# Linear attention with a gated feed-forward: queries over the whole array, and a first chunk with its own order of work

## The chip, the cores and the metric

The kernel runs on one core of one Trainium2 chip. The metric is the device time of the whole kernel in microseconds; lower is better. A core has TensorE (matrix products and transposes), VectorE, ScalarE, GpSimd and SyncE, each with its own instruction stream; in the profile they are PE, DVE, ACT, POOL and SP, and PEld is TensorE's weight load. They meet at semaphores only.

## The reference

x has shape (8, 1024, 256) in fp32. One layer is computed:

```python
xn = layernorm(x)                                    # over the 256 channels
q, k, v = (split_heads(xn @ W.T) for W in (Wq, Wk, Wv))   # 16 heads of 16
q, k = elu(q) + 1, elu(k) + 1
kv_state = einsum('bhnd,bhne->bhde', k, v)
k_state = k.sum(axis=2)
attn = einsum('bhnd,bhde->bhne', q, kv_state) / maximum(einsum('bhnd,bhd->bhn', q, k_state), 1e-6)
local = xp[:, :-2] * conv_w[:, 0] + xp[:, 1:-1] * conv_w[:, 1] + xp[:, 2:] * conv_w[:, 2] + conv_b
y = (attn + local) @ Wp.T + bp
h = silu(xn @ wg.T) * (xn @ wu.T)                    # 768 wide, integer weights times 1/127
out = x + y + h @ wd.T
```

## The kernel before

The 8 x 1024 tokens are worked off in 16 chunks of 512 tokens (4 tiles of 128), two chunks (c = 0, 1) to a batch b. The instruction stream of every engine is written out by hand as one `step(b, c, attend, ahead)` per chunk; b = 2 to 6 are a loop. `past` is false in the very first step only, `attend` is true from batch 1 on, `ahead` in all steps but the last.

For the precise products each fp32 operand is split into a high and a low fp16 half, and three products are summed (high x high, low x high, high x low). The weights are first scaled by powers of two. To find these, VectorE takes maxima over each partition (`weight_maximum`), TensorE transposes a group of them (`turn_maxima`), VectorE reduces across (`across`), TensorE spreads the result to all partitions (`spread_maxima`), and VectorE makes the scales (`powers`, `gate_up_scales`, `down_scales`, `attention_scales`). The integer weights need a low half only if a maximum is over 2048; this is decided at run time.

One step, on TensorE:

1. `project_kv(0)`: keys and values of tiles 0 and 1 (12 matmuls of 512 columns, line 1068). If `attend`, then `query(b-1, c, 0)` and `query(b-1, c, 1)` (line 1023): the queries of the chunk one batch back times the state of that batch. Then `project_kv(1)` and `project_q` (12 matmuls, line 984).
2. `accumulate(0)` and `(1)`: keys times values into the state, with the transposes of the attention result between them (line 1033).
3. `gate_up(0)` to `gate_up(5)` (lines 1119 and 1128, 8 matmuls each), with `project_y` of the chunk one batch back between them, then `down(0)` and `down(1)` (line 1138). gate_up(j) waits until `hid` of j - 2 is made, gate_up(1) until q_relu is read.

Beside it: ScalarE makes k_neg, k_relu, v_sb, k_exp (`key_parts`), q_neg and q_exp (`query_parts`), silu, the high halves and the middle tap of the convolution. VectorE makes the statistics of the next chunk, the attention division (`normalise`), k_sb, q_relu, q_sb, the other taps, y, hid, the low halves, res and out. GpSimd makes rstd, xn and xT, the channel-major fp32 copy for the convolution. The next chunk's xn is split into xn_h and xn_l, which two DMA transposes on SP's queue turn into xh and xl.

The state of a batch is kept for 64 channels at a time: `row_mask` cuts `head_mask` to 64 columns, `state` is 64 + 4 columns per channel block (AW = 68), and a query matmul uses 64 of the array's 128 rows:

```python
for r in range(R):
    rows = slice(r * ROWS, (r + 1) * ROWS)
    cols = slice((i % 2 * KT + k) * AW, (i % 2 * KT + k + 1) * AW)
    ins = nc.tensor.matmul(ps[:, banks[p] + r, cols],
                           q_sb[rows, c, k, i * P:(i + 1) * P], state[rows, k, :],
                           start=True, stop=True, tile_position=(r * ROWS, 0))
```

In the first step, x of chunk 0 comes as one load of 512 KB. TensorE warms up with 24 fp32 matmuls of the identity, does the first group of maxima, and warms up with 16 more (line 992). GpSimd makes all four tiles of xn, these are split and turned by DMA, and the projection is that of every other step.

## Time and profile before

| what | value |
|---|---|
| time, median of 3 runs | 517.81 us (517.47 to 517.92) |
| the profiled execution | 517.49 us, span 515.9 us |
| TensorE busy | 497.8 us, 96% |
| VectorE busy | 435.3 us, 84% |
| ScalarE busy | 333.0 us, 65% |
| GpSimd busy | 132.6 us, 26% |
| granted TensorE clock | 1.000 of full speed (mean) |

The span runs from the first to the last instruction of the profiled execution. Busy time counts an instruction from its start to its end; matmuls overlap in the array, so their single durations are longer than the pace at which they follow each other. The chain of waits is followed back from the last instruction: at each step to what released it, or to the instruction before it on its engine.

### The profile page before, as it was taken

Reading aid. Unit: us, or ns where it says so; the run is one execution under the profiler, and the core shown is the slowest. Engines: PE = TensorE matmul, PEld = TensorE weight load, DVE = VectorE, ACT = ScalarE, POOL = GpSimd, SP = SyncE. Lnnn points to the kernel's source line nnn. Section 1 sums busy time; section 2 is a strip of 40 time slices with the busy share of each in tenths; the row PEclk is TensorE's granted clock in tenths of the full one; section 3 lists DMA queues with packets and bytes.
Section 4 is the critical chain, followed back from the end, with each engine's and each line's share of the span. In section 5 each row is a group of like instructions: output and inputs, shape, how many; then the busy total and the mean of one; then the engine's idle time right before and its main releaser. Section 6 shows DMA issues by size and latency. Waiting matters only on the chain.

```text
span 515.9 us, 11639 instructions
## 1 busy us (share of the span) xinstructions
PE 497.8 (96%) x4249; PEld 302.7 (59%) x4249; DVE 435.3 (84%) x866; ACT 333.0 (65%) x521; POOL 132.6 (26%) x148
## 2 busy tenths in 40 slices
PE   7978989999999999999999999999999999999997
PEld 7435455664747556574755657465564756647576
DVE  4989798878888988888898888888888889887787
ACT  1576767757576674856667485666748577674770
POOL 3151414050231405023140511414041140401050
PEclk9999999999999999999999999999999999999999
DMA  6935424232523523252342425324242442223012
GB/s 234 269 68 113 86 62 103 42 124 42 164 43 83 124 42 122 41 163 41 78 119 37 132 41 141 62 61 121 38 146 41 114 89 41 86 40 83 3 42 81
DMA packets 70750, 45.90 MB, mean 89 GB/s; under 512 B 35520, under 2 KB 70208, under 8 KB 70720
## 3 DMA queue, kind: packets, MB, share of 16 engines
q1 hardware_dynamic: 61728, 36.58, 24.9%
q0 software_dynamic: 8448, 8.39, 10.8%
q10 hardware_dynamic: 544, 0.52, 0.4%
q8 instruction: 20, 0.33, 0.3%
q14 instruction: 10, 0.08, 0.0%
HBM read 20.32 MB, written 8.39 MB: 56 GB/s over the span
## 4 chain that ended last, share of the span: by engine, by line
PE 73%; DVE 12%; issue 7%; ACT 6%; DMA 1%; POOL 1%; DVEq 0%; ACTq 0%
PE ps L1068 16%; PE ps L984 15%; PE ps L1138 15%; PE ps L1119 11%; PE ps L1128 10%; PE ps L1023 5%; ACT q_neg L490 3%; DVE hid L854 3%; DVE y L765 3%; DVE q_sb L823 2%; DMA x_in<-in_L_attn_x_dram 1%; DVE maxima L617 1%; ACT hh L507 1%; DVE bn_raw L557 1%; ACT act_g L499 1%
## 5 line engine op out<-in xcount | busy, mean ns | idle before, releaser
L499 ACT ACTIVATE act_g<-ps,scales 128x512 f32<-128x512 f32 x96 | 66.0, 687 | 46.5 <-PE ps L1128 45.0
L854 DVE SCALAR_TENSOR_TENSOR hid<-act_g,scales,ps 128x512 f32<-128x512 f32 x96 | 71.3, 744 | 26.8 <-ACT act_g L499 26.7
L860 DVE TENSOR_TENSOR hl<-hid,hh 128x512 f16<-128x512 f32 x96 | 66.5, 693 | 1.5
L352 POOL TENSOR_TENSOR xT<-xh,xl 128x1024 f32<-128x1024 f16 x16 | 33.9, 2121 | 123.8 <-DMA xl<-xn_l 111.1
L1119 PE MATMUL ps<-xh,g_wh 128*128 128x512 f16 x192 | 57.6, 382 | 6.2 <-DVE hid L854 5.8
L507 ACT ACTIVATE hh<-hid 128x512 f16<-128x512 f32 x96 | 59.7, 622 | 5.4 <-DVE hid L854 5.4
L466 ACT ACTIVATE k_neg<-ps,scales 128x512 f32<-128x512 f32 x32 | 22.0, 687 | 57.6 <-PE ps L1068 57.6
L1128 PE MATMUL ps<-xl,g_wh 128*128 128x512 f16 x192 | 57.1, 379 | 0.0
L1128 PE MATMUL ps<-xl,u_wh 128*128 128x512 f16 x192 | 57.1, 379 | 0.0
L1119 PE MATMUL ps<-xh,u_wh 128*128 128x512 f16 x192 | 57.1, 379 | 0.0
L440 ACT ACTIVATE local<-xT,cb,cw 128x512 f32<-128x512 f32 x32 | 24.3, 806 | 42.7 <-POOL xT L352 39.4
L1138 PE MATMUL ps<-d_wh,hh 128*128 128x256 f16 x384 | 47.7, 273 | 2.8 <-DVE hid L854 1.8
L322 POOL TENSOR_SCALAR xn<-x_in,neg_mean,rstd 128x256 f32<-128x256 f32 x64 | 48.4, 771 | 4.3 <-POOL rstd L329 4.2
L1138 PE MATMUL ps<-d_wh,hl 128*128 128x256 f16 x384 | 47.5, 273 | 0.0
L791 DVE SCALAR_TENSOR_TENSOR local<-xT,cw,local 128x512 f32<-128x512 f32 x60 | 44.2, 775 | 0.5 <-ACT local L440 0.5
L1138 PEld LDWEIGHTS ps<-d_wh,hh 128*128 128x128 f16 x384 | 36.1, 98 | 9.9 <-ACT hh L507 1.9
L1138 PEld LDWEIGHTS ps<-d_wh,hl 128*128 128x128 f16 x384 | 36.2, 98 | 6.5 <-DVE hl L860 0.3
L870 DVE SCALAR_TENSOR_TENSOR res<-ps,scales,xb 128x512 f32<-128x512 f32 x32 | 23.8, 745 | 18.7 <-PE ps L1138 18.7
L329 POOL TENSOR_TENSOR rstd<-var_eps,half 128x4 f32<-128x4 f32 x15 | 16.9, 1124 | 74.9 <-DVE var_eps L574 74.9
L348 POOL TENSOR_TENSOR xT<-xh,xl 128x2 f32<-128x2 f16 x8 | 1.6, 194 | 130.0 <-DMA xl<-xn_l 112.8
L1023 PEld LDWEIGHTS ps<-state,q_sb 64*128 64x128 f32 x512 | 29.9, 188 | 7.0 <-issue 6.8
L1068 PE MATMUL ps<-kv_wh,xh 128*128 128x512 f16 x128 | 33.0, 380 | 0.4 <-DMA xh<-xn_h 0.4
(133 smaller groups left out, 958.5 us busy)
## 6 DMA issues: line engine op xcount, KB each, us to landing
x_in<-in_L_attn_x_dram SPq DMA_DIRECT2D x16, 512.0 KB, 4.1
xb<-bp_sb SPq DMA_DIRECT2D x16, 512.0 KB, 3.4
xb<-in_L_attn_x_dram POOLq DMA_DIRECT2D x16, 512.0 KB, 5.8
out_dram<-out_sb SPq DMA_DIRECT2D x14, 512.0 KB, 2.9
out_dram<-out_sb SPq DMA_DIRECT2D x4, 256.0 KB, 2.1
wg_int<-in_L_ffn_w_gate_dram SPq DMA_DIRECT2D x1, 768.0 KB, 7.3
wu_int<-in_L_ffn_w_up_dram SPq DMA_DIRECT2D x1, 768.0 KB, 8.7
wd_int<-in_L_ffn_w_down_dram SPq DMA_DIRECT2D x1, 768.0 KB, 4.8
```

Of the source, the lines that this page charges most:

```text
L322: return nc.gpsimd.tensor_scalar(xn[:, i, :], x_in[:, c, i, :], neg_mean[:, c, i:i + 1], rstd[:, c, i:i + 1], ALU.add, ALU.mult)
L499: nc.scalar.activation(act_g[:, j % 2, :], ps[:, gate_bank(j), :], ACT.Silu, scale=silu_in).then_inc(silu_ready, 1)
L507: nc.scalar.activation(hh[:, j, :], hid[:, j % 2, :], ACT.Copy).then_inc(hh_ready, 1)
L791: nc.vector.scalar_tensor_tensor(out=here, in0=xT[:, c, k, side:side + CHUNK], scalar=cw[:, k, side:side + 1], in1=here, op0=ALU.mult, op1 ...
L854: nc.vector.scalar_tensor_tensor(out=hid[:, j % 2, :], in0=act_g[:, j % 2, :], scalar=h_mul, in1=ps[:, gate_bank(j) + 1, :], op0=ALU.mult, ...
L860: nc.vector.tensor_tensor(hl[:, j, :], hid[:, j % 2, :], hh[:, j, :], ALU.subtract).then_inc(hl_ready, 1)
L984: ins = nc.tensor.matmul(dst, stat(s, k), mov(m, k), start=(n == 0 and k == 0), stop=(n == len(TERMS) - 1 and k == KT - 1))
L1023: ins = nc.tensor.matmul(ps[:, banks[p] + r, cols], q_sb[rows, c, k, i * P:(i + 1) * P], state[rows, k, :], start=True, stop=True, tile_po ...
L1068: ins = nc.tensor.matmul(ps[:, 2 * p + i, :], x2[s][:, c, 2 * p + i, k, :], kv_w[m][:, k, :], start=(n == 0 and k == 0), stop=(n == len(TE ...
L1119: nc.tensor.matmul(dst, w[0][:, k, cols], xh[:, c, :, k, :], start=(k == 0), stop=False)
L1128: ins = nc.tensor.matmul(tiles_of(gate_bank(j) + n), w[0][:, k, j * P:(j + 1) * P], xl[:, c, :, k, :], start=False, stop=(k == KT - 1))
L1138: ins = nc.tensor.matmul(ps[:, banks[p], i * D:(i + 1) * D], h[:, j, t], w[:, j, :], start=start and i == 0, stop=stop, skip_group_check=True)
```

## The change

The queries use all 128 rows: `state` holds 128 + 8 columns per channel block, `row_mask` is gone, and a tile and channel block is one matmul of 136 columns in place of two of 68. The division is done for two tiles in one operation.

The first step is written out anew. x of chunk 0 comes in two halves, on SP's queue and on ScalarE's. VectorE makes two tiles of xn and GpSimd the other two; TensorE transposes them in fp32 (`turn_first`), ScalarE copies them into xT, and keys and values are projected in fp32 from xT and the raw weights (`project_first`), with four small matmuls for the maxima between the four tiles. ScalarE makes xh of chunk 0 and GpSimd xl, from xT. The maxima stand in four groups instead of three, each with a bank of its own. k's high half, k_sb, xn_l of chunk 1 and q_sb of chunk 0 go to GpSimd; q_neg, q_exp and q_relu of chunk 0 to ScalarE behind the last hh. The warm-up is 18 matmuls in one piece. The semaphores that no longer count the first chunk's DMA transposes start one step later; these lines are left out below.

```diff
-WARM_UP = (24, 16)
+WARM_UP = 18
-FIRST_X_SPLIT = 3
+FIRST_X_SPLIT = 2
-    AW = ROWS + HPR
+    AW = P + HPB
-        GROUPS = [["k", "v", "q"], ["g", "u"], ["d", "cw", "cb", "p"]]
+        GROUPS = [["k", "v", "q"], ["g", "u"], ["d"], ["cw", "cb", "p"]]
...
 # SP
-            sp.dma_start(x_in[:, 0, :, :], x_v[0]).then_inc(x_loaded[0], 16)
+            sp.dma_start(x_in[:, 0, 0:2, :], x_v[0][:, 0:2, :]).then_inc(first_x[0], 16)
             load_weights("q", wqT, w_raw["q"][:, :, :])
             load_weights("g", wgT, ffn_rows("g", wgT))
             load_weights("u", wuT, ffn_rows("u", wuT))
-            sp.dma_start(bp_sb[:, :], ...).then_inc(bias_in, 16)
-            turn_x(0, 0)
+            sp.dma_start(x_in[:, 1, :, :], x_v[1]).then_inc(x_loaded[1], 16)
+            load_weights("d", wdT, ffn_rows("d", wdT))
             load_weights("p", wpT, w_raw["p"][:, :, :])
-            load_weights("d", wdT, ffn_rows("d", wdT))
...
-            sp.dma_start(x_in[:, 1, :, :], x_v[1]).then_inc(x_loaded[1], 16)
+            sp.dma_start(bp_sb[:, :], ...).then_inc(bias_in, 16)
...
 # GpSimd
-            normalise(0, 0)
-            normalise(0, 1).then_inc(xn_ready, 1)
-            normalise(0, 2)
+            normalise(0, 2).then_inc(xn_ready, 1)
             normalise(0, 3).then_inc(xn_ready, 1)
-            put_xT(0, 0)
-            add_x(0, 0)
+            pool.wait_ge(first_xh, 1)
+            nc.gpsimd.tensor_tensor(xl[:, 0, :, :, :], xT[...], xh[:, 0, :, :, :], ALU.subtract).then_inc(first_xl, 1)
+            pool.wait_ge(scaled[0], 1)
+            nc.gpsimd.tensor_scalar(kv_w[0][:, :, 0:D], w_raw["k"][:, :, :], col(scale_up, "k"), None,
+                                    ALU.mult).then_inc(k_hi, 1)
+            for p in range(2):
+                pool.wait_ge(k_parts, p + 1)
+                nc.gpsimd.tensor_tensor(k_sb[...], k_exp[:, p, :, :], k_relu[:, p, :, :], ALU.add).then_inc(k_ready, 1)
...
 # ScalarE, first
+            act.dma_start(x_in[:, 0, 2:TILES, :], x_v[0][:, 2:TILES, :]).then_inc(first_x[1], 16)
...
-            x_high(0, 0)
-            high(kv_w[0][:, :, 0:D], w_raw["k"][:, :, :], "k", k_hi)
-            high(q_w[0][:, :, :], w_raw["q"][:, :, :], "q", q_hi)
+            for p in range(2):
+                act.wait_ge(first_turned, p + 1)
+                nc.scalar.activation(xT[:, 0, :, 1 + p * PAIR:1 + (p + 1) * PAIR], halves(FIRST_TURNED[p]),
+                                     ACT.Copy).then_inc(first_xT, 1)
+            act.wait_ge(first_xT, 2)
+            nc.scalar.activation(xh[:, 0, :, :, :], xT[...], ACT.Copy).then_inc(first_xh, 1)
...
 # VectorE, the first step
+                if not past:
+                    gate_up_scales()
+                    gate_up_high("g", g_w)
+                    stats(nb, ncx)
+                    weight_maximum("d")
+                    gate_up_low_halves()
+                    hidden(0)
+                    hidden(1)
+                    hidden_low(0)
+                    across(2)
+                    put_state()
+                    hidden(2)
+                    hidden_low(1)
+                    down_scales()
+                    hidden(3)
+                    late_maxima()
+                    hidden_low(2)
+                    hidden(4)
+                    hidden_low(3)
+                    across(3)
+                    hidden(5)
+                    hidden_low(4)
+                    hidden_low(5)
+                    attention_scales()
+                    low(kv_w[1][:, :, 0:D], ...)
+                    low(kv_w[1][:, :, D:2 * D], ...)
+                    down_low_half()
+                    put_res(0, DOWN)
+                    put_res(1, DOWN)
+                    return
...
 # TensorE
             def turn_maxima(g):
                 pe.wait_ge(maxed[g], len(GROUPS[g]))
+                if g == len(GROUPS) - 1:
+                    pe.wait_ge(acc_kept, 1)
+                elif g > 0:
+                    pe.wait_ge(scaled[g - 1], 1)
...
+            def project_first(p, i):
+                pe.wait_ge(first_xT, p + 1)
+                t = 2 * p + i
+                for half, n in enumerate(("k", "v")):
+                    pe.wait_ge(w_in[n], 16)
+                    for k in range(KT):
+                        ins = nc.tensor.matmul(ps[:, t, half * D:(half + 1) * D], xT[:, 0, k, 1 + t * P:1 + (t + 1) * P],
+                                               w_raw[n][:, k, :], start=(k == 0), stop=(k == KT - 1))
+                if i == 1:
+                    ins.then_inc(kv_done, 1)
...
-                        for r in range(R):
-                            rows = slice(r * ROWS, (r + 1) * ROWS)
-                            cols = slice((i % 2 * KT + k) * AW, (i % 2 * KT + k + 1) * AW)
-                            ins = nc.tensor.matmul(ps[:, banks[p] + r, cols],
-                                                   q_sb[rows, c, k, i * P:(i + 1) * P], state[rows, k, :],
-                                                   start=True, stop=True, tile_position=(r * ROWS, 0))
+                        ins = nc.tensor.matmul(ps[:, banks[p] + i % 2, k * AW:(k + 1) * AW], q_sb[:, c, k, i * P:(i + 1) * P],
+                                               state[:, k, :], start=True, stop=True)
...
+                if not past:
+                    project_first(0, 0)
+                    turn_maxima(0)
+                    project_first(0, 1)
+                    spread_maxima(0)
+                    project_first(1, 0)
+                    turn_maxima(1)
+                    project_first(1, 1)
+                    spread_maxima(1)
+                    project_q()
+                    pe.wait_ge(gate_up_hi, 2)
+                    pe.wait_ge(gate_up_seen, 1)
+                    is_wide["gate_up"] = pe.value_load(gate_up_wide[0:1, 0:1].bitcast(I32))
+                    gate_up(0)
+                    accumulate(0)
+                    accumulate(1)
+                    gate_up(1)
+                    turn_maxima(2)
+                    gate_up(2)
+                    spread_maxima(2)
+                    gate_up(3)
+                    gate_up(4)
+                    turn_maxima(3)
+                    gate_up(5)
+                    spread_maxima(3)
+                    pe.wait_ge(d_hi, 1)
+                    pe.wait_ge(down_seen, 1)
+                    is_wide["down"] = pe.value_load(wide[0:1, 2:3].bitcast(I32))
+                    down(0, DOWN)
+                    down(1, DOWN)
+                    return
```

## Rows read from the trace of the kernel before

**Rows 1.** The page, part 1: engine, busy us, share, instructions.

```profile
PE 497.8 (96%) x4249; PEld 302.7 (59%) x4249; DVE 435.3 (84%) x866; ACT 333.0 (65%) x521; POOL 132.6 (26%) x148
```

**Rows 2.** The chain of waits in a middle chunk: start us, us, what.

```profile
135.52 2.59 PE ps L1068 x12
138.10 1.94 PE ps L1023 x32
140.04 2.70 PE ps L1068 x12
...
145.37 1.13 ACT q_neg L490
...
165.96 2.59 PE ps L1068 x12
```

**Rows 3.** The timeline, middle chunks: start us, us, engine, line, operation [idle before].

```profile
135.55 0.75 DVE L870 SCALAR_TENSOR_TENSOR res<-ps,scales,xb 128x512 f32<-128x512 f32 x1 [1.21 <-PE ps L1138]
...
150.96 0.61 PE L1119 MATMUL ps<-xh,g_wh 128*128 128x512 f16 x2 [0.27 <-DVE hid L854]
...
168.48 1.86 PEld L1023 LDWEIGHTS ps<-state,q_sb 64*128 64x128 f32 x32 [0.42 <-issue]
...
171.02 0.76 DVE L748 TENSOR_TENSOR attn<-ps,rden 128x256 f32<-128x256 f32 x2
...
176.96 1.28 DVE L816 TENSOR_SCALAR q_relu<-ps,scales 128x1024 f32<-128x1024 f32 x1 [0.68 <-ACT q_neg L490]
```

**Rows 4.** The chain of waits in the first chunk.

```profile
0.93 4.91 DMA x_in<-in_L_attn_x_dram
...
8.37 1.05 POOL rstd L374
...
9.52 2.19 POOL xn L322 x4
...
15.98 3.33 DVE maxima L617 x2
...
22.26 0.69 ACT k_neg L466
...
24.59 1.52 ACT u_wh L426
...
47.53 5.18 PE ps L1068 x24
```

**Rows 5.** The timeline of TensorE in the first chunk.

```profile
2.74 7.80 PE L992 MATMUL ps<-ident 128*128 128x128 f32 x48 [2.74 <-POOL head_mask L370]
...
11.57 3.65 PEld L992 LDWEIGHTS ps<-ident 128*128 128x128 f32 x32
...
27.14 0.59 PE L1119 MATMUL ps<-xh,g_wh 128*128 128x512 f16 x2 [0.33 <-issue]
...
47.37 1.03 PE L1068 MATMUL ps<-kv_wh,xh 128*128 128x512 f16 x4
```

**Rows 6.** Groups by line and form: busy us, mean ns of one.

```profile
L854 DVE SCALAR_TENSOR_TENSOR hid<-act_g,scales,ps 128x512 f32<-128x512 f32 x96 | 71.3, 744 | 26.8 <-ACT act_g L499 26.7
L352 POOL TENSOR_TENSOR xT<-xh,xl 128x1024 f32<-128x1024 f16 x16 | 33.9, 2121 | 123.8 <-DMA xl<-xn_l 111.1 <-issue 12.7
L466 ACT ACTIVATE k_neg<-ps,scales 128x512 f32<-128x512 f32 x32 | 22.0, 687 | 57.6 <-PE ps L1068 57.6
L1033 PEld LDWEIGHTS ps<-ident,attn 128*128 128x128 f32 x128 | 13.7, 140 | 1.0 <-DVE attn L748 0.4
L397 POOL TENSOR_TENSOR local<-local,k_relu 128x512 f32<-128x512 f32 x2 | 2.5, 1272 | 0.0
```

**Rows 7.** Windows of 2 us: busy of PE, PEld, DVE, ACT, POOL, clock, DMA share, GB/s.

```profile
2.00:4.00 2.00, 1.26 (x6) 1.26 (x7) 0.00 (x0) 1.28 (x1) 0.62 (x2) 1.00 0.78 189
4.00:6.00 2.00, 2.00 (x11) 2.00 (x11) 0.14 (x1) 0.00 (x0) 0.00 (x0) 1.00 1.08 381
```

More of the change, by code:

```diff
@@ L192, in build @@
         x_loaded = [sem(f"x_loaded{c}") for c in range(CB)]
+        first_x = [sem(f"first_x{p}_loaded") for p in range(2)]
+        first_normed, first_turned = sem("first_normed"), sem("first_turned")
+        first_xT, first_xh, first_xl = sem("first_xT"), sem("first_xh"), sem("first_xl")
         out_stored = [sem(f"out_stored{c}") for c in range(CB)]
@@ L386, in step @@
                     layernorm(nb, ncx)
+                    if isinstance(b, int) and b == 0 and c == 0:
+                        for p in range(2):
+                            pool.wait_ge(xn_h_ready, p + 1)
+                            tiles = slice(2 * p, 2 * p + 2)
+                            nc.gpsimd.tensor_tensor(xn_l[:, tiles, :], xn[:, tiles, :], xn_h[:, tiles, :],
+                                                    ALU.subtract).then_inc(xn_l_ready, 1)
+                        add_x(0, 0)
                     add_x(nb, ncx)
-                if ahead:
                     put_xT(nb, ncx)
+                if isinstance(b, int) and b == 0 and c == 0:
+                    pool.wait_ge(q_parts, 1)
+                    pool.wait_ge(q_read, 1)
+                    nc.gpsimd.tensor_tensor(q_sb[:, 0, :, :], q_exp[:, :, :], q_relu[:, :, :],
+                                            ALU.add).then_inc(q_ready, 1)
             run(pool, step)
@@ L553, in stats @@
             def stats(b, c):
-                dve.wait_ge(x_loaded[c], (b + 1) * 16)
+                first = isinstance(b, int) and b == 0 and c == 0
+                if not first:
+                    dve.wait_ge(x_loaded[c], (b + c) * 16)
                 for i in range(TILES):
+                    if first and i % 2 == 0:
+                        dve.wait_ge(first_x[i // 2], 16)
                     nc.vector.bn_stats(bn_raw[:, c, i, :], x_in[:, c, i, :]).then_inc(bn_seen, 1)
@@ L644, in _ @@
             stats(0, 0)
-            for n in ("k", "v", "q"):
-                weight_maximum(n)
+            weight_maximum("k")
+            dve.wait_ge(rstd_ready, 1)
+            for i in range(2):
+                ins = nc.vector.tensor_scalar(xn[:, i, :], x_in[:, 0, i, :], neg_mean[:, 0, i:i + 1],
+                                              rstd[:, 0, i:i + 1], ALU.add, ALU.mult)
+            ins.then_inc(first_normed, 1)
+            weight_maximum("v")
+            weight_maximum("q")
+            weight_maximum("g")
             across(0)
-            x_low(0, 0, 0)
-            x_low(0, 0, 1)
+            weight_maximum("u")
             powers(0)
@@ L917, in step @@
                             x_low(nb, ncx, 1)
-                        if j == 2 and not past:
-                            down_scales()
-                        if j == 3 and past and not attend:
+                        if j == 3 and not attend:
                             projection_scales()
@@ L1109, in gate_up @@
                         pe.wait_ge(v_ready, at(b, c, 2, 2))
+                    elif j == 1 and not past:
+                        pe.wait_ge(v_ready, 1)
                     elif j == 1:
@@ L1165, in step @@
                 project_kv(1)
-                if not past:
-                    spread_maxima(1)
                 project_q()
                 accumulate(0)
-                if not past:
-                    turn_maxima(2)
                 if attend:
@@ L1175, in step @@
                 accumulate(1)
-                if not past:
-                    pe.wait_ge(gate_up_hi, 2)
-                    pe.wait_ge(gate_up_seen, 1)
-                    is_wide["gate_up"] = pe.value_load(gate_up_wide[0:1, 0:1].bitcast(I32))
                 gate_up(0)
-                if not past:
-                    spread_maxima(2)
                 gate_up(1)
```

218 lines of the change are left out of this document (111 added, 107 removed).

## The prediction, made before the change was run

> **What bounds the kernel now.** I read the page first. TensorE is busy for 96% of the span [rows 1], so a change pays if it takes time out of TensorE's stream, or out of a stage in which that stream still waits. Then I read the chain of waits for one chunk in the middle [rows 2]. The reader is to see that from one key/value projection to the next (135.52 to 165.96, 30.44 us) nearly everything is TensorE. The exception is the piece from 145.34 to 150.96, where the chain runs over ScalarE's q_neg and VectorE's q_relu, y, q_sb and hid(0) while TensorE works on accumulations and the first two gate_up. TensorE itself is idle there for 0.27 us only [rows 3]. The queries (line 1023) stand ahead of that piece, between the two halves of the key/value projection. What they save moves the second half, the query projection, q_neg and all that follows, one for one, until VectorE binds. VectorE still waits 0.68 us for q_neg [rows 3], so a few tenths of a microsecond fit under it.
>
> Last I read the first 48 us, in which TensorE is not full. The chain there [rows 4] goes x load, statistics, rstd on GpSimd, xn, splitting, DMA transposes, the maxima of g and u, half of the key/value projection, u's conversion, and from 27.14 the six gate_up and the down projection. The second chunk's projection starts at 47.37 by TensorE's records [rows 5] (the chain counts it from 47.53). That stage is rebuilt by the change.
>
> **Part 1, the queries.** Today a chunk has 4 tiles x 2 channel blocks x 2 row halves = 16 matmuls, which the trace shows as 32 load/multiply passes, so an fp32 matmul is two passes. The chain gives them 1.94 us, and the half projection behind them takes 2.70 us where the same 12 matmuls elsewhere take 2.59 [rows 2]. So the block costs 1.94 + 0.11 = 2.05 us; a pass takes about 0.056.
>
> After the change there are 8 matmuls, 16 passes, over all 128 rows and with 136 moving columns instead of 68. No row shows this. The nearest are the warm-up matmuls: fp32, full array, 128 columns. In the second batch 32 loads take 3.65 us [rows 5], the last one 0.14 of it (a load of this shape [rows 6]), so a pass takes 3.51 / 31 = 0.113 us. If the moving columns set this, 136 of them take 0.120; if load and multiply follow each other, less is added. I take 0.120: 16 x 0.120 = 1.92 us. If the 0.11 behind the block goes, 0.13 us is saved in each chunk; if it stays, 0.02. I take the middle, 0.08. Below, the cost is bounded by the case in which no load hides behind a multiply (rival 1); above, a saving over 0.25 us would need passes under 0.113, which the warm-up excludes. There are 14 steps with queries between the two half projections: 14 x 0.08 = 1.1 us.
>
> The Trainium skill (TensorEngine Tiling (Array Packing), Key Properties) says that a change of tiling mode drains TensorE. Here the 0.11 us behind the row-tiled block agrees in kind; by that rule all of it would go, and the 14 steps would save 1.8 us instead of 1.1.
>
> On VectorE, the two attn operations of a pair (128x256, 0.76 us for the two [rows 3]) become one of 128x512, which by the other 128x512 operations that read the result memory takes about 0.70 (a hid takes 0.744 [rows 6]). That is 0.0 to 0.1 saved per pair, covered in the steady chunks. At the end of the kernel four such pairs lie on VectorE's chain; with two more query blocks I take 0.3 us for the end (0 to 0.6). The state grows from 2 x 64 to 2 x 128 columns once per batch, some 0.1 us on VectorE, and sits ahead of a wait of 1.2 us for the down projection [rows 3]; without that cover it would cost 0.8 us in all.
>
> **Part 2, the first chunk.** I rebuild its chain from durations of before.
> - x load [rows 4]: two halves of 256 KB go first on two queues instead of 512 KB on one beside the weights. The DMA moves 189 GB/s in 2 to 4 us and 381 after [rows 7]: 524 KB are in at 4.0 + 0.4 = 4.4 us, against 5.84.
> - Statistics to rstd: 5.84 to 9.42 [rows 4], so 3.6 us: done at 8.0.
> - xn: GpSimd's four tiles took 2.19 us [rows 4]; now two are there, 1.1 us, and two on VectorE beside it: 9.1.
> - TensorE's warm-up: 36 passes. The 48 took 7.80 [rows 5], and 12 of the fast kind less are 6.4: over at 9.15, so the transposes wait for neither for long.
> - Transposes and copies: 8 passes of about 0.12 = 1.0 us. The copy of the first half by ScalarE (as k_neg, 0.69 [rows 6]) runs 9.7 to 10.4. This replaces the splitting and the two DMA transposes on the chain; for the first chunk two DMA issues leave SP's queue, and the weights d and p, x of chunk 1 and the bias are issued some 10 us sooner, behind u, so they delay nothing ahead of them.
> - Key/value projection in fp32: 4 tiles x 2 x 2 = 16 matmuls of 256 columns, 32 passes. A pass lies between 0.113 + 0.054 = 0.167 (only the extra 128 columns, at the fp16 matmuls' 2.59 / 12 for 512 [rows 2]) and 2 x 0.113 = 0.227. I take 0.22, since fp32 columns seem to set the warm-up's pace too: 7.0 us, against 2 x 2.6 = 5.2 in fp16. With the small matmuls for maxima between, put at three passes' time each for two of them and their waits, 0.7 us: 10.4 to 18.1.
> - ScalarE's four operations on the second pair took 22.26 to 24.59, 2.3 us, then u's conversion 1.5 [rows 4]: 18.1 + 2.3 + 1.6 = 22.0, gate_up(0) at 22.2 against 27.14 [rows 4]: 4.9 us sooner.
>
> Two side paths must be earlier. VectorE: maxima of k, v, q, then g and u (1.7 us each [rows 4]) end at about 14.7, the first scales stand at 15.8, the second at 19.4 (they wait for the small matmul queued behind the last projection, 18.5), g's conversion at 20.4: under 22.0, by 1.6 us. GpSimd: the low half of x, 2.1 us as its xT [rows 6], ends at 14.5; then k's conversion and two k_sb of 1.3 each [rows 6], the second waiting for k_exp at 20.4, end at 21.7.
>
> From gate_up(0) to the next chunk's projection before took 47.37 - 27.14 = 20.2 us. After, both accumulations (0.8 us) stand inside; VectorE's late maxima and down_scales move into the loop as well, but statistics, q_relu and q_sb of chunk 0 leave it: the last two go to ScalarE and GpSimd behind the loop. I set these equal. So the head saves 4.9 - 0.8 = 4.1 us. The moved query parts take ScalarE, with a table load, four operations of some 1.15 (q_neg takes 1.13 [rows 2]), 4.6 us from about 38.1, done at 42.7, when the middle taps need it; VectorE's scales and low halves end about 43, before the third term of chunk 1 needs them.
>
> What is late next: turn_maxima(3) waits for p, cw and cb in the middle of the gate_up loop, and spread_maxima(2) for VectorE's across(2); gate_up(3) and gate_up(5) are queued behind them. My walk through the order has TensorE wait some 0.9 us at each, about what it waited before. If both double, the head saves 2.3; if no such wait shows and passes take 0.167, some 6.
>
> **Sum.** The profiled execution took 517.49 us (span 515.9, 1.6 around it; the median of the runs is 517.81, 0.3 above). 517.5 - 4.1 - 1.1 - 0.3 = 512.0 us.
>
> **Rivals.**
> 1. *Slower: full-array loads don't hide.* The row halves of today may let one half's load run under the other's multiply. If on the full array each fp32 load stands ahead of its multiply, a pass is the 0.120 of moving columns plus a load, 0.054 by the pace of today's loads [rows 3]: 0.174 x 16 = 2.8 us, 0.75 more per chunk, over 14 steps and the end 11 to 12 us. With the head's 4.1: 517.5 - 4.1 + 11.5 = 525 us. It outweighs the head from 4.1 / 15 = 0.27 us per chunk, a pass of (2.05 + 0.27) / 16 = 0.145. The Trainium skill (TensorE: Matmul & The Clock Gate, Part 3, The mechanism) states that a weight load overlaps matmuls in flight only where the row group differs, which speaks for this rival. Against it: the warm-up is just such a stream and already needs only 0.113 with its loads, and fp16 matmuls run at 2.59 / 12 = 0.216 with a load for each. Chance 6%.
> 2. *The head gives nothing:* fp32 passes, the scales' new order and waits behind the small matmuls eat what the earlier x brings. Then 517.5 - 1.4 = 516.1; with queries at 0.02 instead, 516.9, within the bound of no change. For it: VectorE, busy 84% of the span [rows 1], carries nearly all side paths above, and one late link shifts all. Against: the splitting and the DMA transposes are surely off the chain of the first chunk. Chance 14%.
> 3. *The queries give more:* the drain goes and loads hide so well that a chunk saves 0.2: 517.5 - 4.1 - 2.8 - 0.6 = 510.0. Chance 15%.
> 4. *The forecast:* 65%, with its own range 510 to 514.5.
>
> **Numbers.** The range reaches to rival 3 with a head of 5.3 below (508.8) and into rival 2 above (516.6); rival 1 and the far end of 2 stay outside, with some tail below. A measurement of this kernel can tell about 0.2%, 1.0 us, from no change. Faster by more: the forecast, rival 3 and two thirds of rival 2, 0.88. Same: the rest of rival 2 and small misses, 0.05. Slower: rival 1 and a head that loses, 0.07.
>
> **What would show it.** In the changed kernel's trace: 16 passes of line query in about 1.9 us per chunk and 2.6 us for the half projection behind them; period of a chunk 30.3 to 30.4; x in at 4.4; the first fp32 projection matmul at 10.4 and the last ending at 18; gate_up(0) at 22.2; chunk 1's projection at 43.2. The prediction is wrong if a query pass takes over 0.13, if VectorE instead of ScalarE's u conversion releases gate_up(0), or if TensorE's idle time in the gate_up loop of the first chunk grows by over 2 us.

## The result, and the profile after

The changed kernel takes 515.62 us (median of 6 executions, 515.18 to 515.88), the kernel before 517.86 (6 executions, 517.47 to 518.09): a ratio of 0.9957, 95% interval 0.9944 to 0.997. It is faster, and the time lies in the range given, but the gain is 2.2 us where the sum had 4.1 + 1.1 + 0.3 = 5.5. The profiled execution took 515.18 us, span 513.6 (before: 515.9).

The page of the changed kernel, part 1, answers to [rows 1]: TensorE has 281 matmul records and 5 us of busy time less, VectorE 3 us less, GpSimd 11.5 us more.

```profile
PE 492.7 (96%) x3968; PEld 304.8 (59%) x3968; DVE 432.5 (84%) x833; ACT 334.4 (65%) x522; POOL 144.1 (28%) x152
```

**The queries.** The chain of waits of the changed kernel in a middle chunk (start us, us, what) answers to [rows 2]:

```profile
135.63 2.59 PE ps L1140 x12
138.22 1.85 PE ps L1096 x16
140.07 2.59 PE ps L1140 x12
...
165.90 2.16 PE ps L1140 x10
```

The query block is 1.85 us instead of 1.94, a pass 1.85 / 16 = 0.116. The half projection behind it is 2.59 instead of 2.70: all of the 0.11 has gone. From one chunk's projection to the next it is 165.90 - 135.63 = 30.27 us instead of 30.44 [rows 2].

**The first chunk.** The timeline of TensorE in the changed kernel (start us, us, engine, line, operation, idle time before it) answers to [rows 5]:

```profile
10.06 1.13 PE L1080 MATMUL ps<-wk_raw,xT 128*128 128x256 f32 x4 [0.25 <-ACT xT L459]
...
11.89 0.27 PE L1051 MATMUL ps<-ident,maxima 128*3 128x128 f32 x1
...
23.17 0.59 PE L1197 MATMUL ps<-xh,g_wh 128*128 128x512 f16 x2 [1.42 <-ACT u_wh L455]
...
44.38 1.03 PE L1140 MATMUL ps<-kv_wh,xh 128*128 128x512 f16 x4
...
47.68 1.04 PE L1140 MATMUL ps<-kv_wl,xh 128*128 128x512 f16 x4 [1.41 <-DVE kv_wl L675]
...
55.19 0.46 PE L1159 MATMUL ps<-v_sb,k_sb 128*32 128x33 f32 x32 [0.90 <-DVE k_sb L846]
...
71.33 0.39 PE L1216 MATMUL ps<-d_wh,hl 128*128 128x256 f16 x2 [0.73 <-DVE hl L900]
...
74.78 1.03 PE L1140 MATMUL ps<-kv_wh,xh 128*128 128x512 f16 x4
```

The reader is to subtract these starts from those of before. The first gate_up starts at 23.17 instead of 27.14: 3.97 us sooner. Chunk (0,1)'s projection starts at 44.38 instead of 47.37: 2.99 sooner. Chunk (1,0)'s starts at 74.78, and before it started at 74.42, as the timeline of TensorE in the kernel before has it:

```profile
74.42 1.03 PE L1068 MATMUL ps<-kv_wh,xh 128*128 128x512 f16 x4
```

So the whole lead of the first chunk is given back within the second one, and 0.36 us more. It goes in two places: the accumulation of chunk (0,1) (line 1159) starts at 55.19, and in the kernel before at 56.11, so 2.99 us of lead have become 0.92 there; the other 1.28 us go between it and (1,0). What takes it is seen on VectorE and GpSimd, in the timeline of the changed kernel:

```profile
40.92 0.16 DVE L754 SCALAR_TENSOR_TENSOR scales<-power,scales 128x1 f32<-128x1 f32 x1
41.11 1.98 DVE L756 SCALAR_TENSOR_TENSOR scales<-power,scales 128x1 f32<-128x1 f32 x1
...
44.09 2.22 DVE L766 TENSOR_SCALAR cw<-cw_raw,scales 128x6 f32<-128x6 f32 x1
46.22 0.74 DVE L675 SCALAR_TENSOR_TENSOR kv_wl<-wk_raw,scale_up,kv_wh 128x512 f16<-128x512 f32 x1
...
47.55 1.40 DVE L910 SCALAR_TENSOR_TENSOR res<-ps,scales,xb 128x512 f32<-128x512 f32 x2
...
68.76 3.12 DVE L900 TENSOR_TENSOR hl<-hid,hh 128x512 f16<-128x512 f32 x2 [0.38 <-ACT hh L544]
...
40.94 2.14 POOL L361 TENSOR_TENSOR xT<-xh,xl 128x1024 f32<-128x1024 f16 x1
43.94 2.34 POOL L416 TENSOR_TENSOR q_sb<-q_exp,q_relu 128x1024 f32<-128x1024 f32 x1 [0.86 <-ACT q_relu L583]
...
68.60 2.12 POOL L361 TENSOR_TENSOR xT<-xh,xl 128x1024 f32<-128x1024 f16 x1 [9.26 <-issue]
```

L754 and L756 are the same operation on a 128x1 column; one takes 0.16 us, the other 1.98, and it ends (43.09) when GpSimd's xT does (43.08). L766 takes 2.22 instead of 0.23 (its time in run 3 below) and ends with q_sb, at 46.3. The two hl take 3.12 us, where two take 1.47 in the kernel before, because the first ends only with the next xT; TensorE waits 0.73 us for it. Each time a VectorE operation is held until a GpSimd operation that began earlier is over. The two low halves kv_wl, for which TensorE waits 1.41 us, stand behind two such holds. The Trainium skill (SBUF — State Buffer, Who interferes with whom) states this: a VectorE instruction with two inputs in SBUF contends with a GpSimd instruction that reads SBUF, one in a two-port mode contends with GpSimd as well, and the one that issues first has the ports for its whole length while the other stands still. The trace agrees, with the 1.98 us for a column of 128 numbers.

The kernel before had the same hold, in its timeline of VectorE and GpSimd:

```profile
44.06 2.08 DVE L709 SCALAR_TENSOR_TENSOR scales<-power,scales 128x1 f32<-128x1 f32 x1
...
47.47 1.40 DVE L870 SCALAR_TENSOR_TENSOR res<-ps,scales,xb 128x512 f32<-128x512 f32 x2
...
44.01 2.12 POOL L352 TENSOR_TENSOR xT<-xh,xl 128x1024 f32<-128x1024 f16 x1
```

That TensorE came to chunk (0,1) only at 47.37 hid it there. The two res lines tell what sets this stage: VectorE reaches res of the first chunk at 47.47 before and at 47.55 after. TensorE has a lead of 3 us at this place, VectorE has none, and from here TensorE needs what VectorE makes. Run 4 below shows it in another way.

### The profile page after: what moved, and what is told of

Read it like the earlier page. It is cut to its first block, busy times and chain, and to the rows that moved or that the text cites. A ratio compares the mean times of both kernels' runs of the same rounds, so it can differ in the third digit from the quotient of the medians.

```text
span 513.6 us, 11017 instructions
## 1 busy us (share of the span) xinstructions
PE 492.7 (96%) x3968; PEld 304.8 (59%) x3968; DVE 432.5 (84%) x833; ACT 334.4 (65%) x522; POOL 144.1 (28%) x152
## 4 chain that ended last, share of the span: by engine, by line
PE 72%; DVE 13%; issue 7%; ACT 5%; DMA 2%; DVEq 0%; ACTq 0%
PE ps L1034 15%; PE ps L1216 15%; PE ps L1140 14%; PE ps L1197 11%; PE ps L1206 11%; PE ps L1096 5%; ACT q_neg L526 3%; DVE hid L894 3%; DVE y L804 3%; DVE q_sb L863 2%; DMA wv_raw<-in_L_attn_Wv_dram 2%; DVE maxima L663 1%; DVE hl L900 1%; ACT act_g L536 1%; DVE local L830 1%
## 5 line engine op out<-in xcount | busy, mean ns | idle before, releaser
L900 DVE TENSOR_TENSOR hl<-hid,hh 128x512 f16<-128x512 f32 x96 | 68.2, 711 | 1.7 <-ACT hh L544 0.4
L361 POOL TENSOR_TENSOR xT<-xh,xl 128x1024 f32<-128x1024 f16 x15 | 31.8, 2122 | 110.2 <-issue 110.2
L499 ACT ACTIVATE k_neg<-ps,scales 128x512 f32<-128x512 f32 x30 | 20.6, 687 | 53.1 <-PE ps L1140 53.1
L326 POOL TENSOR_SCALAR xn<-x_in,neg_mean,rstd 128x256 f32<-128x256 f32 x62 | 51.7, 846 | 4.3 <-POOL rstd L333 4.2
L1216 PE MATMUL ps<-d_wh,hh 128*128 128x256 f16 x384 | 47.5, 273 | 2.3 <-ACT hh L544 2.2
L1096 PEld LDWEIGHTS ps<-state,q_sb 128*128 128x128 f32 x256 | 32.1, 190 | 2.9 <-DVE hid L894 0.6
L1096 PE MATMUL ps<-state,q_sb 128*128 128x136 f32 x256 | 32.5, 279 | 0.3 <-DVE hid L894 0.3
```

The lines of the kernel that those rows point to most:

```text
L326: return nc.gpsimd.tensor_scalar(xn[:, i, :], x_in[:, c, i, :], neg_mean[:, c, i:i + 1], rstd[:, c, i:i + 1], ALU.add, ALU.mult)
L900: nc.vector.tensor_tensor(hl[:, j, :], hid[:, j % 2, :], hh[:, j, :], ALU.subtract).then_inc(hl_ready, 1)
L1096: ins = nc.tensor.matmul(ps[:, banks[p] + i % 2, k * AW:(k + 1) * AW], q_sb[:, c, k, i * P:(i + 1) * P], state[:, k, :], start=True, stop= ...
L1216: ins = nc.tensor.matmul(ps[:, banks[p], i * D:(i + 1) * D], h[:, j, t], w[:, j, :], start=start and i == 0, stop=stop, skip_group_check=True)
```

## The experiments

In each profile the time from the start of chunk (1,0)'s projection to the end of the span is 441.5 us with the old queries and 438.7 to 438.8 with the new ones. So that one start, on TensorE's timeline, tells the first two chunks from the rest; the last column gives it. Each ratio is to executions of the kernel before on the same chip (medians 517.69 to 517.86).

The starts scatter too. Up to the first gate_up all kernels with the new head do the same, yet it starts at 23.17 in the changed kernel's profile, the earliest, and at 23.31 to 23.89 in the others. So for these kernels it is safer to count (1,0) from the first gate_up: 51.61 us in the changed kernel, 50.52 in run 3, 50.38 in run 4, 49.38 in run 6.

| kernel | time, us | ratio to before (95%) | span | (1,0) starts |
|---|---|---|---|---|
| before | 517.86 | | 515.9 | 74.42 |
| changed | 515.62 | 0.9957 (0.9944, 0.997) | 513.6 | 74.78 |
| queries only | 514.65 | 0.9942 (0.9929, 0.9956) | 513.0 | 74.34 |
| first chunk only | 518.04 | 1.0005 (0.9996, 1.0014) | 516.7 | 75.22 |
| q_sb on VectorE | 514.45 | 0.9938 (0.9924, 0.9952) | 512.8 | 74.05 |
| xT(1,0) later | 514.16 | 0.9933 (0.9919, 0.9946) | 512.5 | 73.78 |
| these two | 513.3 | 0.9918 (0.9905, 0.9931) | 511.5 | 72.71 |
| these two, and add_x early | 513.2 | 0.9914 (0.9901, 0.9926) | 511.3 | 72.57 |
| low halves first | 516.35 | 0.9975 (0.9964, 0.9985) | 514.8 | 76.04 |
| add_x early alone | 517.1 | 0.9982 (0.9972, 0.9993) | 515.4 | 76.69 |
| both xT later | 515.54 | 0.9952 (0.994, 0.9964) | 514.2 | 75.52 |

**1. Queries only**, the first chunk as before:

```diff
-    AW = ROWS + HPR
+    AW = P + HPB
...
-                        for r in range(R):
-                            rows = slice(r * ROWS, (r + 1) * ROWS)
...
+                        ins = nc.tensor.matmul(ps[:, banks[p] + i % 2, k * AW:(k + 1) * AW], q_sb[:, c, k, i * P:(i + 1) * P],
+                                               state[:, k, :], start=True, stop=True)
```

> The kernel before with the change's queries, state and division, and nothing else of it. Theory A (the queries give all of the gain that was measured, 0.17 us per chunk as the two chains show, 0.20 us in the block): 14 steps and the end save 2.3 to 2.8 us, 515.1 to 515.6, ratio 0.995. Theory B (the queries give what was forecast, 1.1 + 0.3, and the head the rest): 516.5, ratio 0.9973.

The chain of waits of this kernel, in the middle chunk:

```profile
137.67 1.85 PE ps L1007 x16
```

514.65 us: this half of the change alone gains 3.1 us, more than the whole change. It starts chunk (1,0) at 74.34, within 0.1 us of before.

**2. First chunk only**, that is the changed kernel with the old queries (edit 1 undone).

> The changed kernel with the queries, state and division of before. Theory A (the first chunk's gain of 3 us at the second chunk's projection is given back in the second chunk): 517.5 to 518.3, ratio 1.000. Theory B (the head gives 1 to 2 us): 516 to 516.8, ratio 0.997.

518.04 us, not to be told from before, and its profile starts chunk (1,0) at 75.22, 0.8 later than before. The two halves give -3.1 and +0.3, together -2.8, against the -2.2 of the whole change; the 0.6 between is inside the intervals, each of which reaches some 0.5 to 0.7 us to either side. The first chunk's new order gives nothing; this is rival 2, and a little beyond it.

**3. q_sb on VectorE.** Less work beside VectorE's list, but more on it:

```diff
 # GpSimd, end of its first step
-                if isinstance(b, int) and b == 0 and c == 0:
-                    pool.wait_ge(q_parts, 1)
-                    pool.wait_ge(q_read, 1)
-                    nc.gpsimd.tensor_tensor(q_sb[:, 0, :, :], ...).then_inc(q_ready, 1)
 # VectorE, first step, behind down_low_half()
+                    put_q()
```

> The changed kernel with q_sb of chunk 0 made by VectorE ahead of its res operations instead of by GpSimd. Theory A (a VectorE operation that reads only SBUF stands still while a GpSimd operation runs; the cw operation of 2.22 us was held by q_sb): cw takes 0.2 us, the low halves of k and v end about 2 us sooner, TensorE's wait of 1.41 us for them goes, in exchange for 1.2 us more work on VectorE behind; the kernel takes 0.3 to 1.2 us less than the changed one, if the later VectorE chain of the second chunk doesn't eat it. Theory B (the cw operation is long for another reason, DMA traffic or a semaphore): cw stays at 2.2 us and the kernel gets no faster, or 0.5 to 1 us slower by the added work.

The timeline of VectorE and TensorE in this kernel:

```profile
40.89 1.80 DVE L654 TENSOR_SCALAR scale_up<-scale_up 128x3 f32<-128x3 f32 x1
...
44.27 0.23 DVE L761 TENSOR_SCALAR cw<-cw_raw,scales 128x6 f32<-128x6 f32 x1
...
47.76 1.02 PE L1136 MATMUL ps<-kv_wh,xh 128*128 128x512 f16 x4 [0.32 <-DVE res L905]
```

cw is back at 0.23 us, while scale_up, which now stands beside xT, is held in its place (1.80 us), and TensorE no longer waits for the low halves; 0.32 us for res is left of the 1.41. The q_sb that VectorE now makes costs it 1.2 us and the hold had cost it 2.0. 514.45 us, 1.2 less than the changed kernel; from the first gate_up to (1,0) 50.52 instead of 51.61, 1.09 less.

**4. xT of chunk (1,0) later**, behind VectorE's last low half of chunk (0,1):

```diff
+                    if isinstance(b, int) and b == 0 and c == 1:
+                        pool.wait_ge(hl_ready, 2 * J)
                     put_xT(nb, ncx)
```

> The changed kernel, but in the second step GpSimd's xT waits until VectorE has made all low halves of the hidden layer. Theory A (the two low halves took 3.12 us instead of 1.4 because xT ran beside them): they take 1.4 us again, the down projection of chunk 1 is not held, the third chunk starts 1.0 to 1.5 us sooner and the kernel takes that less than the changed one: 514.2 to 514.7. Theory B (chunk 1 is bound by ScalarE's hh, which comes late there, and VectorE's time is only hidden behind it): low halves 1.4 us, but the third chunk starts at the same time within 0.3 us.

The timeline of VectorE, GpSimd and TensorE, and a window (busy of PE, PEld, DVE, ACT, POOL, granted clock, DMA share, GB/s):

```profile
69.04 1.29 DVE L902 TENSOR_TENSOR hl<-hid,hh 128x512 f16<-128x512 f32 x2 [0.38 <-ACT hh L546]
...
70.50 2.32 DVE L880 TENSOR_TENSOR state<-whole_acc,head_mask 128x256 f32<-128x256 f32 x1
...
70.42 2.12 POOL L361 TENSOR_TENSOR xT<-xh,xl 128x1024 f32<-128x1024 f16 x1 [10.83 <-DVE hl L902]
...
46.31 1.03 PE L1142 MATMUL ps<-kv_wh,xh 128*128 128x512 f16 x4
```

```profile
41.00:42.00 1.00, 1.00 (x7) 0.69 (x6) 0.93 (x3) 0.97 (x2) 1.00 (x3) 0.50 1.23 194
```

The two hl take 1.29 us instead of 3.12. The hold has not gone, it has moved to the state (2.32 us instead of 0.42), for which nobody waits yet. 514.16 us, 1.5 less than the changed kernel. From the first gate_up to (1,0) it is 50.38 instead of 51.61, 1.23 less, and all of that lies behind the accumulation of chunk (0,1): from there to (1,0) it takes 18.35 us, the changed kernel 19.59, the kernel before 18.31.

This profile shows something more. The granted clock was 0.50 from about 40.3 to 43.7 us, and chunk (0,1) starts at 46.31, 1.93 us later than in the changed kernel. Its accumulation starts at 55.43, only 0.24 later (from the first gate_up 32.03 us, the changed kernel 32.02), and TensorE no longer waits for the low halves. The execution took 514.16 us, the four with a mean clock of 1.000 took 514.01 to 514.57. So nearly two microseconds of TensorE's lead at this place are worth nothing: VectorE's list sets when the stage ends.

**5. Three moves**: 3 and 4, and GpSimd's add_x of both chunks issued ahead of its xn_l, so that the transposes' data would not queue behind it.

```diff
+                        add_x(0, 0)
+                        add_x(0, 1)
                         for p in range(2):
                             pool.wait_ge(xn_h_ready, p + 1)
...
-                        add_x(0, 0)
-                    add_x(nb, ncx)
+                    else:
+                        add_x(nb, ncx)
```

> The changed kernel with three moves that keep VectorE and GpSimd apart: q_sb of chunk 0 on VectorE, the second step's xT behind the hidden layer's low halves, and the two adding loads of x issued ahead of GpSimd's low half of xn, so that the DMA transposes aren't behind them and the first step's xT comes sooner. Theory A (each held operation was on the path at its own place): the two gains measured, 1.2 and 1.5 us, add up and the third brings up to 1 more, 512.0 to 513.0. Theory B (they overlap, since the second chunk is bound by VectorE once the first hold goes): 513.3 to 514.2.

**6. Moves 3 and 4 together**, without that of add_x.

> The changed kernel with q_sb(0,0) on VectorE and the xT of chunk (1,0) behind the low halves of the last hidden pair; the add of x stays where the change has it. Theory A (each held VectorE operation costs what TensorE waits for it, and the two places are far enough apart to add): 515.6 - 1.2 - 1.5 = 512.9 us, at most 0.3 from the version with all three moves (513.2). Theory B (the head's lead is given back by a chain that later work limits anyway, so that the second move finds what the first has already given): 514.0 or more, near the better of the two alone (514.2).

513.2 and 513.3 us: the two holds add up, roughly by the medians (1.2 + 1.5 = 2.7 expected, 2.3 measured) and closely by the profiles, counted from the first gate_up (1.09 + 1.23 = 2.32 expected, 51.61 - 49.38 = 2.23 measured). The move of add_x gives nothing. Both kernels beat the one before, the changed one, and the queries alone. The timeline of TensorE with three moves shows what is left of the head:

```profile
43.68 1.03 PE L1140 MATMUL ps<-kv_wh,xh 128*128 128x512 f16 x4
...
47.52 1.02 PE L1140 MATMUL ps<-kv_wh,xh 128*128 128x512 f16 x4 [0.85 <-DVE res L909]
...
54.27 0.46 PE L1159 MATMUL ps<-v_sb,k_sb 128*32 128x33 f32 x32 [1.02 <-DVE k_sb L845]
```

Chunk (0,1) starts 3.69 us sooner than before, chunk (1,0) at 72.57, 1.85 sooner. Most of the other 1.84 us are TensorE's waits for VectorE, 0.85 for res and 1.02 for k_sb, where before it waited 0.41 for k_sb and not at all for res. VectorE's list still has a hold in it: scale_up takes 1.80 us beside xT here, as in run 3.

**7. Low halves first**: the changed kernel with kv_wl ahead of `attention_scales`.

```diff
+                    low(kv_w[1][:, :, 0:D], ...)
+                    low(kv_w[1][:, :, D:2 * D], ...)
                     attention_scales()
-                    low(kv_w[1][:, :, 0:D], ...)
-                    low(kv_w[1][:, :, D:2 * D], ...)
```

> The changed kernel with VectorE's low halves of k and v ahead of the attention scales instead of behind them; GpSimd is left as it is. Theory A (what counts at chunk 1 is when VectorE has finished its whole list, which the two held operations set, not the wait of TensorE for the low halves alone): TensorE's wait of 1.41 us moves to the res operation or to k_sb behind it, and the kernel gains under 0.5 us: 515.1 to 515.9. Theory B (the wait for the low halves itself is the loss): 514.0 to 514.6.

The timeline of VectorE and TensorE:

```profile
41.15 2.62 DVE L675 SCALAR_TENSOR_TENSOR kv_wl<-wv_raw,scale_up,kv_wh 128x512 f16<-128x512 f32 x1
...
44.68 2.18 DVE L754 SCALAR_TENSOR_TENSOR scales<-power,scales 128x1 f32<-128x1 f32 x1
...
49.62 1.02 PE L1140 MATMUL ps<-kv_wh,xh 128*128 128x512 f16 x4 [1.95 <-DVE res L910]
```

516.35 us, 0.7 slower than the changed kernel. TensorE gets its low halves in time and waits 1.95 us for res instead, since two holds of the same size now fall on other operations of the same list. This order doesn't help: as theory A had it, the wait moves to res. That the kernel gets slower, by 0.7, was in neither theory, and why is open; VectorE stands idle for 0.45 us ahead of res here and doesn't in the changed kernel.

**8. add_x early alone.**

> The changed kernel with only the two adding loads of x moved ahead of GpSimd's low half of xn. Theory A (the low half's DMA transpose took 6.5 us because 1 MB of adding loads ran beside it): it lands in 3 to 4 us, the first step's xT starts about 3 us sooner and meets a hidden low half instead of the attention scales; the scale operation takes 0.2 us instead of 2 and the kernel takes 0.3 to 1.5 us less, 514.1 to 515.3. Theory B: landing unchanged, time unchanged within 0.3 us.

The timeline of TensorE and VectorE, then a window (columns as in run 4):

```profile
48.16 1.12 PE L1142 MATMUL ps<-kv_wl,xh 128*128 128x512 f16 x4 [2.16 <-DVE kv_wl L677]
49.08 1.91 PE L1142 MATMUL ps<-kv_wh,xh 128*128 128x512 f16 x4
...
44.60 2.84 DVE L677 SCALAR_TENSOR_TENSOR kv_wl<-wk_raw,scale_up,kv_wh 128x512 f16<-128x512 f32 x1
```

```profile
50.00:52.00 2.00, 2.00 (x6) 0.69 (x5) 2.00 (x6) 1.66 (x5) 0.00 (x0) 0.50 0.66 231
```

The transposes didn't land sooner for it: GpSimd's xT begins at 40.74, and in the profiles without this move it begins anywhere from 39.55 (run 6) to 41.18 (run 4). q_sb now holds kv_wl itself, TensorE stands still for 2.16 us, and behind this wait the granted clock is 0.50, the 1.2 GHz level: four matmuls take 1.91 us instead of 1.03. Of the 12 executions the nine with a mean granted clock of 0.997 took 516.94 to 517.64 us, the three at 1.0 took 514.79 to 515.98. So the edit itself costs nothing, and the fall of the clock some 2 us. That the wait brings the fall isn't shown: the waits of 1.41 (changed kernel) and 1.95 us (run 7) were not followed by one, and the fall in run 4 came some 0.9 us behind a wait of 1.18, which the changed kernel has too (1.17), without a fall. Where the clock falls decides the price: in run 4, where TensorE had a lead, it cost nothing.

**9. Both xT later**: three moves, and xT of chunk (0,1) waits for q_sb, so that nothing stands beside VectorE's list.

```diff
+                    if isinstance(b, int) and b == 0 and c == 0:
+                        pool.wait_ge(q_ready, 1)
```

> The version with three moves, and GpSimd starts xT of chunk (0,1) only when VectorE's q_sb(0,0) is written (about 46 us), so that no GpSimd operation stands beside VectorE's list of scales and low halves. Theory A (the hold of 1.6 us on the scales at 40.66 delays all behind it): the list ends some 1.6 us sooner, TensorE's wait for res (0.85 us) goes, and the time falls by 0.8 to 1.0 us to about 512.3. Theory B (something else ends that stretch: the taps, which need xT, or k_sb, for which TensorE waits 1.02 us): within 0.3 us of 513.2, or above it if the taps now wait for xT.

The timeline of VectorE, GpSimd and TensorE:

```profile
45.78 1.40 DVE L911 SCALAR_TENSOR_TENSOR res<-ps,scales,xb 128x512 f32<-128x512 f32 x2
49.25 1.46 DVE L831 SCALAR_TENSOR_TENSOR local<-xT,cw,local 128x512 f32<-128x512 f32 x2 [2.07 <-ACT local L474]
...
46.25 2.12 POOL L361 TENSOR_TENSOR xT<-xh,xl 128x1024 f32<-128x1024 f16 x1
...
51.68 0.60 PE L1036 MATMUL ps<-xh,q_wh 128*128 128x512 f16 x2 [2.07 <-ACT v_sb L512]
```

The hold has gone, res comes 0.85 us sooner (45.78 against 46.63 with three moves), and TensorE's wait for it too. But the taps now wait 2.07 us for xT, ScalarE, which makes the middle tap first, is late with v_sb, and TensorE waits 2.07 us for that; the clock falls to 0.50 again. 515.54 us; the one execution of six with the clock at 1.0 took 513.74. Even so it is no better than 513.2: the second theory, in its worse form. The run takes the hold away only by making xT late (46.25, where it starts at 40.31 in run 5), so it doesn't tell what the stage would take with neither.

**10. The pace of fp32 passes.** The changed kernel, in one execution of which only the pace is read (544.99 us). Behind the warm-up stand five series of 24 more fp32 matmuls (48 passes each), whose results nobody reads: full array with 128, 64 and 32 columns, and two with 64 rows.

```diff
             warm(WARM_UP)
+            for _ in range(24):
+                nc.tensor.matmul(ps[:, 3, 0:P], ident[:, :], ident[:, 0:P], start=True, stop=True)
+            for _ in range(24):
+                nc.tensor.matmul(ps[:, 3, 0:64], ident[:, :], ident[:, 0:64], start=True, stop=True)
+            for n in range(24):
+                r = 64 * (n % 2)
+                nc.tensor.matmul(ps[:, 3 - n % 2, 0:64], ident[r:r + 64, :], ident[r:r + 64, 0:64],
+                                 start=True, stop=True, tile_position=(r, 0))
...
```

> The changed kernel with five series of 24 extra fp32 matmuls of the identity behind the warm-up, into banks that are free then: A full array with 128 moving columns, B full array with 64, C halves of 64 rows in turn with 64 columns, D always the same half of 64 rows with 64 columns, E full array with 32. Only their pace is read; the head comes some 10 us later. Theory A (an fp32 pass is set by its moving columns, two cycles each, loads hidden): 0.11, 0.057, 0.057, 0.057 and 0.05 or less for the last, where the load of 128 columns sets it. Theory B (load and multiply follow each other, as rival 1 has it, unless row groups differ): A 0.11, B 0.085, C 0.06, D 0.085, E 0.07.

The timeline of TensorE, and two windows (columns as in run 4):

```profile
8.59 5.52 PE L1087 MATMUL ps<-ident 128*128 128x128 f32 x48
13.95 5.47 PE L1089 MATMUL ps<-ident 128*128 128x64 f32 x48
19.35 2.90 PE L1092 MATMUL ps<-ident 64*128 64x64 f32 x48
22.08 6.07 PE L1095 MATMUL ps<-ident 64*128 64x64 f32 x48
28.08 10.45 PE L1098 MATMUL ps<-ident 128*128 128x32 f32 x48
```

```profile
26.00:27.00 1.00, 1.00 (x11) 1.00 (x11) 0.00 (x0) 0.00 (x0) 0.00 (x0) 0.94 0.00 0
27.00:28.00 1.00, 1.00 (x6) 0.96 (x5) 0.00 (x0) 0.00 (x0) 0.00 (x0) 0.50 0.00 0
```

A series takes from its start to that of the next. Full array, 128 columns: 5.36 / 48 = 0.112 us a pass; 64 columns: 5.40 / 48 = 0.112, the same. Two halves in turn: 2.73 / 48 = 0.057; always the same half: 6.00 us, of which some 1.1 at half clock, so about (4.9 + 0.55) / 48 = 0.113. 32 columns at half clock: 10.26 / 48 = 0.214, or 0.107 at full. So on the full array a pass has a floor of about 0.11 us which the columns don't lower, and only halves in turn go below it. Neither theory had this: each took the columns to set the pace of at least one of the series.

## Why the prediction was right in its direction and wrong in its size

**The failed step is that of the side paths in part 2: "VectorE's scales and low halves end about 43, before the third term of chunk 1 needs them".** They end at 47.6, 1.4 us too late, and what lies behind them is late as well. Two things were missing in that step. The list was costed as if GpSimd's work beside it were free; its two holds cost 1.8 + 2.0 us, and a third one (hl, 1.8) comes in chunk (0,1), where it costs TensorE 1.2. The row that should have told it was in the trace of before, the 2.08 us of L709 beside 2.12 us of L352, and the prediction didn't use it: it moved k's high half, k_sb, xn_l and q_sb to GpSimd without asking what they would lock. Second, TensorE's lead was carried into the sum as the kernel's, though VectorE, which TensorE needs from 47 us on, reaches res at 47.5 in both. The head was to give 4.1 us and cost 515.62 - 514.65 = 1.0 over the queries alone, a gap of 5.1 by the medians. By the starts in the profiles it was to give 4.1 and has -0.36 at (1,0), a gap of 4.46, in three parts: 1.11 are missing at chunk (0,1)'s start already (2.99, not 4.1), 2.07 go from there to the accumulation of chunk (0,1), and 1.28 from there to (1,0). The last part is the hold on hl; runs 4 and 6 take it away whole (18.35 and 18.31 us against 19.59). Of the second, run 6 gives back 0.79 (its accumulation starts at 54.40). The other 1.28 I put down to VectorE's list, in which the hold beside xT still stands, from the waits that runs 5 and 6 still show; no run took them away.

**A hold inside the gate_up loop was overlooked as well.** The timeline of VectorE in the changed kernel:

```profile
32.67 1.01 DVE L738 TENSOR_TENSOR scales<-scales,power 128x1 f32<-128x1 f32 x1
```

It takes 1.01 us beside the xn_l (31.27 to 33.66) that the change gave to GpSimd, where its like takes 0.15 in the kernel before, and it lies on the chain of waits, ahead of the maxima for which TensorE waits 1.00 us. It takes 1.01 in the profiles of runs 2 to 9 too, so what it costs isn't known.

**The signs named in the prediction did not catch this.** A query pass takes 0.116 us, ScalarE's u conversion releases gate_up(0), and TensorE's waits in the gate_up loop and ahead of the down projection add up to 3.4 us, where they were 3.5. From gate_up(0) to chunk (0,1) it takes 21.21 us where 20.2 + 0.8 = 21.0 were forecast. None of the three signs of being wrong came up, and none of them looks at the second chunk, where most of the loss lies.

**Up to the first gate_up the steps were right.** x is in at 4.18 (4.4 forecast), rstd done at 7.72 (8.0), the first fp32 projection starts at 10.06 (10.4), a pass takes (11.89 - 10.06) / 8 = 0.229 us (0.22), the last ends at 18.75 (18.1), and gate_up(0) starts at 23.17 (22.2). Of this last miss of 1.0 us, 0.58 is "issue" on the chain of waits, between the end of u's conversion and the first matmul; there the program has TensorE's value load, which was left out. Chunk (0,1) starts at 44.38 (43.2). GpSimd's holds act here too, in small: the spread of the first maxima, in the timeline of the changed kernel,

```profile
11.68 2.08 POOL L389 TENSOR_TENSOR xl<-xT,xh 128x1024 f16<-128x1024 f32 x1 [2.60 <-ACT xh L462]
...
12.96 0.82 DVE L647 TENSOR_SCALAR spread<-ident,group_max 3x3 f32<-3x3 f32 x1
```

takes 0.82 us instead of 0.22 and ends with xl.

**The queries' term was mis-sized, 1.4 us with the end where run 1 measured 3.1.** The mechanism was right: 16 passes, loads that hide, a drain behind the block. The pass takes 0.116, not 0.120, and the 0.11 behind the block goes in full, where the middle was taken: 2.05 - 1.85 = 0.20 on the chain, 0.17 in the period. From chunk (1,0) to the end that makes 441.5 - 438.8 = 2.7 us. This is rival 3's mechanism. The Trainium skill (TensorEngine Tiling (Array Packing), Key Properties) has the drain at a change of tiling mode; by it the 14 steps would save 1.8, nearer to what was measured than the 1.1 taken.

**Rival 1 was false.** A load does run beside a multiply on the full array: 16 query passes with their loads take 1.85 us. The rule of the Trainium skill (TensorE: Matmul & The Clock Gate, Part 3, The mechanism) that loads overlap only where the row group differs does not fit these rows (the same section also lets a load into the background weight buffer go ahead, which they don't contradict), in which a pass of 136 columns takes 0.116 us and one of 64 columns 0.112; it fits only in that halves in turn are twice as fast (0.057). **Rival 2 was what happened to the head**, and for the reason given in its favour, a late link in VectorE's side paths; rival 3 happened to the queries. The sum had the head 5.1 us too good and the queries and the end 1.7 too poor, so the two errors partly cancel. That 515.62 still lies in the range is luck to that extent: with the queries at their forecast and the head as measured it would have been 517.5 - 1.4 + 1.0 = 517.1, outside it.

## What to carry to other kernels

Before work moves to GpSimd, list which VectorE operations will run beside it and read two inputs from SBUF, or are tensor_scalar operations on SBUF. Each can be held for the whole GpSimd operation, here two microseconds for a column of numbers, and a hold that is harmless in the kernel before stops being so when the stage behind it comes forward. When a chain is shortened on one engine, ask at its end where the other engines stand: a lead that VectorE doesn't share lasts until the next thing that VectorE must deliver. And put a long GpSimd operation where VectorE's held work isn't waited for; here one such move was worth 1.2 us by the profiles and 1.5 by the medians (run 4).

## What the runs showed of the hardware

- Not every VectorE operation is held. Two res, which read their first input from the result memory, take 1.40 us beside an xT (run 9), as everywhere else. A reduction that starts 0.39 us into an xT takes its usual 1.74 (kernel before, at 17.57), and a reciprocal on 128x3 0.18 (run 5, at 40.45). Held were tensor_tensor and scalar_tensor_tensor on two SBUF inputs down to 128x1, and tensor_scalar on one SBUF input with two to six columns, in fp32 (128x3: 1.80 us, run 3) and in int32 (128x3: 1.90, run 6). A tensor_scalar on 128x1 was not: 0.15 us each beside xn_l (changed kernel, 31.45 to 32.7). In the middle chunks k_sb starts while GpSimd's xn run, of 0.9 us each; some take 0.68 us as alone, others up to 1.00 (changed kernel, at 142.80).
- The hold goes the other way too. In run 6 the xT that starts at 39.55, while VectorE's two hl run (38.69 to 40.16), takes 2.59 us instead of 2.12.
- An fp32 pass on the full array takes 0.112 us with 128 and with 64 columns (run 10), 0.116 with 136 and 0.229 with 256 (changed kernel).
- In run 10 the granted clock went from 1.00 to 0.50 (the 1.2 GHz level) at about 26.9 us while TensorE had no gap in its records since 2.74 us: before the fall it ran fp32 passes of 64 columns, the last 5 us on one half of the rows. It was back at 1.00 in the window from 44 us. Why it fell is open.
